# Masks added on VectorE in a fused add-and-extreme step, the causal matmuls left out, and the order table made anew

## The chip, the cores and the metric

The kernel runs on one core of a Trainium2 chip. The metric is the device time of one execution in microseconds (us): the median of three runs before the change is 4441.46 us (4438.94 to 4445.67). All five engines matter here: PE (TensorE, the matmuls), DVE (VectorE), ACT (ScalarE), POOL (GpSimd) and SP (which issues the transfers).

## The reference, cut to what matters

64 independent examples (`b`), each of 128 rows (`s`) by 256 features, pass through four layers. They hold five attentions of 16 heads, numbered 0 to 4 in the kernel: attention 0 is causal, attention 2 adds a mask that is an input of the kernel.

```
def _mha(x, kv, Wq, Wk, Wv, mask, causal):          # attentions 0 (causal) and 1
    ...
    energy = jnp.einsum('bhsk,bhtk->bhst', Q, K)
    lengths = jnp.sum(energy[:, :, 0, :] != 0, axis=-1)
    energy = jnp.where(cols[None, None, None, :] >= lengths[:, :, None, None], -jnp.inf, energy)
    if causal:
        energy = jnp.where(cols[None, :] > cols[:, None], -jnp.inf, energy)
    score = jax.nn.softmax(energy / jnp.sqrt(dk), axis=-1)
    ...
# layer 1 (attention 2, heads 64 wide, rotary, then a gated MLP)
scores = jnp.einsum('bhqd,bhkd->bhqk', q, k) / math.sqrt(HD)
scores = scores + attention_mask
probs = jax.nn.softmax(scores, axis=-1)
...
# layer 2 (attention 3): plain softmax.  layer 3 (attention 4): scaled, clipped at +-50, softmax
```

## The kernel before, in words

All weights stay in SBUF. Each example is a chain of about 85 steps ("events"), from the transposition of its input (`xT`) to its last normalization (`norm` 4). Every event is named by a name, the attention or layer `a` and, where an attention is cut in four units of four heads, the unit `u`: `scores` is the product of queries and keys of all 16 heads on PE; `soft` the maximum (DVE) and the exponential (ACT) of one unit; `turn` the transposition of one unit's probabilities (PE) and its copy (ACT); `values` the product with the values; `attended` the transposition back (PE) and the division by the sums (DVE); `first_row` finds the length penalty (`pen`); `prob_norm` divides the probabilities of attention 2 (reciprocal on DVE, product on POOL); `kv2`, `q2`, `o2`, `gate`, `up`, `down`, `z`, `h` are the projections of the layers.

Four examples are under way at once (four slots of every buffer). The order is written out by hand: the table `LIFE` (from L76) gives each event a number for each engine that takes part, and `order(engine)` (L170) sorts the events of all examples by `PERIOD * b + number`. `PERIOD` and the numbers only set this order. On each engine the instructions run strictly in it; between engines there are semaphores. So in the middle of the run the same sequence comes again for each example, on each engine, with steps of four examples interleaved. Of PSUM, four banks (`scores_ps`) hold the scores of one attention, and four (`gen_ps`) go round for all else: a step on PE waits until the bank that was filled four steps earlier has been read.

The masking of attention 0 on PE: `scores` (L519) first multiplies the identity by a bfloat16 table of the causal mask, four matmuls of 512 columns (L537); then come the penalties (16 matmuls, L542) and the scores (L563) into the same banks. In `scores_out` (L932) DVE takes the maximum of one unit (128x512, four heads) straight from PSUM, negated, for attentions 0, 1 and 3 (L957); for attention 2 it adds the mask into `masked` in SBUF (L944) and takes the maximum from there (L946). In `exponentials` (L708) ACT reads attention 0, 1 and 3 from PSUM (L724) and attention 2 from `masked` (L721), head by head, with the negated maximum as its bias. `masked` has three places, and DVE waits on each unit for the exponential of three units earlier (`exp_done`). The score banks are free for the next attention when the last unit is `scored` (after attentions 2 and 4) or `exp_done` (after 0, 1 and 3).

Of the kernel before, what the change touches and what calls it, by code (L numbers as in the profile page):

```python
# [73 lines left out]
PERIOD = 66.01  # L74

LIFE = [  # L76
    ("xT", 0, 0, {"PE": 0.00, "ACT": 2.67, "DVE": 14.33}),
# [1125 lines left out]
```

## Time and profile before

| | |
|---|---|
| profiled execution | 4448.31 us |
| its span, first to last instruction | 4446.5 us |
| PE busy | 4086.8 us (92%) |
| DVE busy | 2928.1 us (66%) |
| ACT busy | 2694.5 us (61%) |
| POOL busy | 1233.9 us (28%) |
| granted TensorE clock | 0.990 of full speed |
| chain that ended last | PE 42%, DVE 40%, issue 10%, POOL 5% |

Busy is the share of the span in which an engine works; the rest is waiting for others. The chain that ended last is followed back from the last instruction, at each step to what released it. Transfers play no part after the start: they move 53 MB in all, at 12 GB/s on average.

### The profile page before, as it was taken

What the parts mean: (1) busy time and instruction counts of PE and PEld (TensorE: products, weight loads), DVE (VectorE), ACT (ScalarE), POOL (GpSimd) and SP (SyncE); (2) the same over time, 40 slices, a digit from 0 to 9 for tenths busy, and PEclk for the clock granted to TensorE, in tenths of its full rate; (3) what the DMA queues carried; (4) which work ended last, traced back from release to release, by engine and by line L of the source; (5) the groups of instructions that cost most, each with busy time, mean ns of one, the idle gap of its engine ahead of it and who ended that gap; (6) DMA issues with size and microseconds to landing.
All of it is one profiled execution on the core that took longest, in us unless ns stands there. A gap on an engine that the chain in (4) does not pass through costs nothing.

```text
span 4446.5 us, 116614 instructions
## 1 busy us (share of the span) xinstructions
PE 4086.8 (92%) x45024; PEld 3473.5 (78%) x45024; DVE 2928.1 (66%) x7395; ACT 2694.5 (61%) x8513; POOL 1233.9 (28%) x2247
## 2 busy tenths in 40 slices
PE   4899999999999999999999999999999999999996
PEld 3778778787787787787787887787787877877875
DVE  2576676676666666766766766766766766766664
ACT  2566666656656656656656666666666666566563
POOL 0232322322322322323323323323223223223221
PEclk8999999999999999999999999999999999999998
DMA  3000000000000000000000000000000000000000
GB/s 122 1 11 7 11 11 6 11 11 7 11 11 6 11 11 6 11 11 7 11 9 8 11 6 11 11 6 11 11 6 11 11 6 11 11 6 11 11 3 5
DMA packets 47341, 52.92 MB, mean 12 GB/s; under 512 B 5328, under 2 KB 46288, under 8 KB 46416
## 3 DMA queue, kind: packets, MB, share of 16 engines
q1 hardware_dynamic: 46800, 45.46, 3.2%
q8 instruction: 369, 6.05, 0.5%
q14 instruction: 172, 1.41, 0.1%
HBM read 37.05 MB, written 8.39 MB: 10 GB/s over the span
## 4 chain that ended last, share of the span: by engine, by line
PE 42%; DVE 40%; issue 10%; POOL 5%; ACT 2%; DVEq 0%; DMA 0%; POOLq 0%; ACTq 0%
PE gen_ps L481 25%; PE gen_ps L473 9%; DVE negmax L957 4%; DVE masked L944 4%; POOL rstd L779 4%; DVE masked L951 4%; PE gen_ps L598 3%; DVE st L919 2%; DVE xs L929 2%; DVE zn L914 2%; ACT prob L724 2%; PE gen_ps L587 2%; PE scores_ps L556 2%; DVE negmax L946 2%; PE scores_ps L563 1%
## 5 line engine op out<-in xcount | busy, mean ns | idle before, releaser
L481 PE MATMUL gen_ps<-actT,w_sb 128*128 128x128 f32 x11264 | 1394.5, 277 | 3.4 <-ACT actT L694 3.3
L481 PEld LDWEIGHTS gen_ps<-actT,w_sb 128*128 128x128 f32 x11264 | 1325.8, 193 | 23.0 <-ACT actT L694 6.2
L724 ACT ACTIVATE prob<-scores_ps,negmax 128x128 f32<-128x128 f32 x3072 | 859.8, 406 | 330.6 <-DVE negmax L957 330.6
L779 POOL TENSOR_TENSOR rstd<-ve,consts 128x1 f32<-128x1 f32 x448 | 282.9, 631 | 1525.0 <-DVE ve L921 1000.0
L473 PE MATMUL gen_ps<-consts,prob 128*128 128x128 f32 x4096 | 591.0, 279 | 65.1 <-ACT prob L724 63.1
L694 ACT ACTIVATE probT<-gen_ps 128x512 f32<-128x512 f32 x1024 | 585.8, 638 | 59.7 <-PE gen_ps L473 59.7
L473 PEld LDWEIGHTS gen_ps<-consts,prob 128*128 128x128 f32 x4096 | 467.8, 142 | 184.9 <-ACT prob L724 147.2
L957 DVE TENSOR_REDUCE negmax<-scores_ps 128x4 f32<-128x512 f32 x768 | 492.0, 682 | 82.7 <-PE scores_ps L563 82.2
L481 PE MATMUL gen_ps<-w_sb,actT 128*128 128x256 f32 x2048 | 532.3, 383 | 2.7 <-ACT actT L694 1.9
L481 PE MATMUL gen_ps<-w_sb,wide 128*128 128x256 f32 x2048 | 467.9, 381 | 1.2 <-issue 1.2
L694 ACT ACTIVATE actT<-gen_ps 128x256 f32<-128x256 f32 (+1 forms) x576 | 276.5, 480 | 301.4 <-PE gen_ps L473 294.0
L832 POOL TENSOR_SCALAR prob<-prob,rden 128x128 f32<-128x128 f32 x1024 | 363.4, 376 | 233.4 <-DVE rden L987 233.4
L481 PEld LDWEIGHTS gen_ps<-w_sb,wide 128*128 128x128 f32 x2048 | 378.9, 190 | 55.6 <-ACT wide L694 1.6
L721 ACT ACTIVATE prob<-masked,negmax 128x128 f32<-128x128 f32 x1024 | 396.3, 394 | 0.0
L481 PEld LDWEIGHTS gen_ps<-w_sb,actT 128*128 128x128 f32 x2048 | 353.0, 193 | 31.7 <-ACT actT L694 3.6
L694 ACT ACTIVATE oT<-gen_ps 128x512 f32<-128x512 f32 x256 | 152.1, 594 | 347.2 <-PE gen_ps L587 347.2
L951 DVE TENSOR_TENSOR masked<-scores_ps,mask 128x512 f32<-128x512 f32 x256 | 175.7, 686 | 175.5 <-PE scores_ps L556 175.4
L716 ACT ACTIVATE probT<-masked 128x512 f32<-128x512 f32 x256 | 161.7, 632 | 212.5 <-DVE masked L954 212.4
L587 PE MATMUL gen_ps<-probT,v 128*32 128x128 f32 x8192 | 279.9, 278 | 11.0 <-ACT probT L716 6.5
L587 PEld LDWEIGHTS gen_ps<-probT,v 128*32 128x32 f32 x8192 | 210.4, 110 | 59.2 <-ACT actT L694 20.2
L787 POOL TENSOR_TENSOR res<-zn,xs 128x256 f32<-128x256 f32 x64 | 46.6, 727 | 737.7 <-DVE zn L914 737.7
L473 PE MATMUL gen_ps<-consts,zn 128*128 128x128 f32 x640 | 132.3, 289 | 127.9 <-DVE zn L914 77.3
(125 smaller groups left out, 5737.9 us busy)
## 6 DMA issues: line engine op xcount, KB each, us to landing
ctx_rms<-x_dram SPq DMA_DIRECT2D x64, 128.0 KB, 2.2
ctx<-ctx_dram SPq DMA_DIRECT2D x64, 128.0 KB, 2.2
mask<-mask_dram SPq DMA_DIRECT2D x128, 64.0 KB, 2.0
out_dram<-res SPq DMA_DIRECT2D x64, 128.0 KB, 1.7
w_sb<-weights_dram SPq DMA_DIRECT2D x1, 7680.0 KB, 25.9
w_sb<-weights_dram SPq DMA_DIRECT2D x1, 2048.0 KB, 30.3
rows_sb<-rows_dram SPq DMA_DIRECT2D x1, 1408.0 KB, 8.2
consts<-consts_dram SPq DMA_DIRECT2D x1, 460.5 KB, 3.3
```

The source lines that it names most:

```text
L473: last = nc.tensor.transpose(ps[:, k * P:(k + 1) * P], src, ident)
L481: last = nc.tensor.matmul(ps, lhsT(c), rhs(c), start=(c == 0), stop=(c == chunks - 1))
L587: last = nc.tensor.matmul(ps[32 * k:32 * k + 32, u * S:(u + 1) * S], v16[:, b % G, HU * u + k, :], probT[:, u, k, :], start=True, stop=True)
L694: release(nc.scalar.activation(dst, take(act, name, b)[:, 0:width], ACT.Copy), name, b)
L716: nc.scalar.activation(probT[:, N % 4, :, :], masked[:, N % 3, :, :], ACT.Exp).then_inc(sem("exp_done"), 1)
L721: ins = nc.scalar.activation(prob[:, N % 4, k, :], masked[:, N % 3, k, :], ACT.Exp, bias=negmax[:, N % 4, k:k + 1], accum_out=den[:, N % 4 ...
L724: ins = nc.scalar.activation(prob[:, N % 4, k, :], scores_ps[:, u, k * S:(k + 1) * S], ACT.Exp, bias=negmax[:, N % 4, k:k + 1])
L779: nc.gpsimd.tensor_tensor(dst, src, const("expo")[:, 0:width], ALU.pow)\
L832: ins = nc.gpsimd.tensor_scalar(prob[:, N % 4, k, :], prob[:, N % 4, k, :], rden2[:, N % 4, k:k + 1], 0.0, ALU.mult, ALU.add)
L944: link(nc.vector.tensor_tensor(masked[:, N % 3, :, :], ps, mask1[:, g, :].unsqueeze(1).to_broadcast([P, HU, S]), ALU.add))
L951: link(nc.vector.tensor_tensor(masked[:, N % 3, :, :], ps, fT[:, g, :].unsqueeze(1).to_broadcast([P, HU, S]), ALU.mult))
L957: ins = nc.vector.tensor_reduce(negmax[:, N % 4, :], ps, AX.X, ALU.max, negate=True)
```

## The change

For attentions 0 and 2 DVE now works head by head: one fused instruction computes -(scores + mask) for 128x128 elements, writes it to `masked` and gathers its minimum, which is the negated maximum of the masked scores and goes to `negmax`. The mask is the causal table for attention 0 and the input's mask for attention 2. ACT takes the exponential of both from `masked`, with the scale -1. The causal matmuls and their bfloat16 tables go; the first penalty matmul of a bank now starts the sum in it. The score banks are also free at `scored` after attention 0. All numbers of the order table are new; two of its lines stand for them here.

```diff
-PERIOD = 66.01
+PERIOD = 68.67
 LIFE = [
-    ("soft", 0, 0, {"ACT": 40.04, "DVE": 32.01}),
+    ("soft", 0, 0, {"ACT": 45.98, "DVE": 51.83}),
 ...
-                eng.wait_ge(sem("scored") if last in (2, 4) else sem("exp_done"), U * k)
+                eng.wait_ge(sem("exp_done") if last in (1, 3) else sem("scored"), U * k)
 ...
-                if a == 0:
-                    for r in range(R):
-                        nc.tensor.matmul(scores_ps[:, r, :], identb[:, :],
-                                         causalb[:, :].unsqueeze(1).to_broadcast([P, HU, S]),
-                                         start=True, stop=False, skip_group_check=True)
                 for k in range(HU if a < 2 else 0):
                     for r in range(R):
                         nc.tensor.matmul(scores_ps[:, r, k * S:(k + 1) * S], pick[rows_of(r), k, :],
-                                         pen[rows_of(r), g, :], start=(a == 1 and k == 0), stop=False,
+                                         pen[rows_of(r), g, :], start=(k == 0), stop=False,
 ...
-                    if a == 2:
+                    if a == 0:
                         ins = nc.scalar.activation(prob[:, N % 4, k, :], masked[:, N % 3, k, :], ACT.Exp,
+                                                   bias=negmax[:, N % 4, k:k + 1], scale=-1.0)
+                    elif a == 2:
+                        ins = nc.scalar.activation(prob[:, N % 4, k, :], masked[:, N % 3, k, :], ACT.Exp, scale=-1.0,
                                                    bias=negmax[:, N % 4, k:k + 1], accum_out=den[:, N % 4, k:k + 1])
 ...
-                if a == 2:
-                    if u == 0:
+                if a in (0, 2):
+                    if a == 2 and u == 0:
                         dve.wait_ge(mask1_sem(b), 16 * (b // G + 1))
-                    link(nc.vector.tensor_tensor(
-                        masked[:, N % 3, :, :], ps, mask1[:, g, :].unsqueeze(1).to_broadcast([P, HU, S]), ALU.add))
-                    ins = nc.vector.tensor_reduce(negmax[:, N % 4, :], masked[:, N % 3, :, :], AX.X, ALU.max,
-                                                  negate=True)
+                    for k in range(HU):
+                        ins = nc.vector.tensor_tensor_reduce(
+                            out=masked[:, N % 3, k, :], in0=ps[:, k, :], in1=mask1[:, g, :] if a else const("causal"),
+                            scale=-1.0, scalar=3.4e38, op0=ALU.add, op1=ALU.min,
+                            accum_out=negmax[:, N % 4, k:k + 1])
```

In the order, place one: DVE at `soft` of attention 2, before. L860 is the end of `norm` 0, L987 the reciprocal of `prob_norm`, L908 begins `attended` 3.

```order
L860 TENSOR_SCALAR live<-absmax 128x1
L944 TENSOR_TENSOR masked<-scores_ps,mask 128x512
L946 TENSOR_REDUCE negmax<-masked 128x4
L944 TENSOR_TENSOR masked<-scores_ps,mask 128x512
L946 TENSOR_REDUCE negmax<-masked 128x4
L944 TENSOR_TENSOR masked<-scores_ps,mask 128x512
L946 TENSOR_REDUCE negmax<-masked 128x4
L944 TENSOR_TENSOR masked<-scores_ps,mask 128x512
L946 TENSOR_REDUCE negmax<-masked 128x4
L987 RECIPROCAL rden<-den 128x4
L908 RECIPROCAL rden<-gen_ps 128x16
L914 TENSOR_TENSOR zn<-gen_ps,rden 128x256
```

Each unit is an addition and a reduction.

The same place now, its first unit only (L854 is the old L860). ISA is the fused instruction, and the second ISA, of 128x1, the read of what it gathered.

```order
L854 TENSOR_SCALAR live<-absmax 128x1
L939 ISA masked,negmax<-scores_ps,mask 128x128
L939 ISA negmax 128x1
L939 ISA masked,negmax<-scores_ps,mask 128x128
L939 ISA negmax 128x1
L939 ISA masked,negmax<-scores_ps,mask 128x128
L939 ISA negmax 128x1
L939 ISA masked,negmax<-scores_ps,mask 128x128
L939 ISA negmax 128x1
L993 BN_STATS cst<-ctx 128x6
L994 BN_AGGR cmv<-cst 128x2
L995 TENSOR_SCALAR cve<-cmv 128x1
```

Two instructions a unit have become eight, with `ctx_norms` (L993 on) moved in between the units.

Place two: PE from `queries` and `keys` of attention 1 (the second and third row) to its scores (L563), before. The row with `zn` is `zT` 3, the one with `mask` `mask4`, the one with `q` `first_row` 1, the 128x256 behind it `o` 3, the ones with `prob` `turn` 2, and `xs` and `ctx` `tr` 4.

```order
L473 MATMUL gen_ps<-consts,ctx_rms 128x128 x2
L481 MATMUL gen_ps<-actT,w_sb 128x128 x8
L481 MATMUL gen_ps<-w_sb,actT 128x256 x2
L473 MATMUL gen_ps<-consts,zn 128x128 x2
L473 MATMUL gen_ps<-consts,mask 128x128
L481 MATMUL gen_ps<-plainT,q 128x128 x2
L481 MATMUL gen_ps<-w_sb,actT 128x256 x2
L473 MATMUL gen_ps<-consts,prob 128x128 x8
L473 MATMUL gen_ps<-consts,xs 128x128 x2
L473 MATMUL gen_ps<-consts,ctx 128x128 x2
L542 MATMUL scores_ps<-pen,pick 128x128 x16
L563 MATMUL scores_ps<-plainT,wide 128x128 x16
```

The same place now (L477 is the old L481, L469 the old L473, L533 and L554 are the old L542 and L563).

```order
L477 MATMUL gen_ps<-actT,w_sb 128x128 x8
L477 MATMUL gen_ps<-w_sb,actT 128x256 x2
L469 MATMUL gen_ps<-consts,mask 128x128
L477 MATMUL gen_ps<-actT,w_sb 128x128 x4
L477 MATMUL gen_ps<-w_sb,actT 128x256 x2
L469 MATMUL gen_ps<-consts,zn 128x128 x2
L469 MATMUL gen_ps<-consts,prob 128x128 x4
L477 MATMUL gen_ps<-plainT,q 128x128 x2
L477 MATMUL gen_ps<-w_sb,actT 128x256 x2
L469 MATMUL gen_ps<-consts,prob 128x128 x4
L533 MATMUL scores_ps<-pen,pick 128x128 x16
L554 MATMUL scores_ps<-plainT,wide 128x128 x16
```

`tr` 4 has moved behind the scores, `keys` 0 (the fourth and fifth row) ahead of `turn` 2, `zT` 3 directly ahead of it, and one unit of `turn` 2 now stands ahead of `first_row` 1, which was first.

Place three: PE from the scores of attention 0 to `zT` 4, before. The row with `probT` is `values` 4, the one with `xs` `x2T`, the one of 20 the second halves of `gate` and `up` and `h`, the 128x256 behind it `z`, the one with `oT` `attended` 4, with `prob` `turn` 0, with `wide` `down`, with `zn` `zT` 4.

```order
L537 MATMUL scores_ps<-causalb,identb 128x512 x4
L542 MATMUL scores_ps<-pen,pick 128x128 x16
L563 MATMUL scores_ps<-plainT,wide 128x128 x16
L587 MATMUL gen_ps<-probT,v 32x128 x16
L473 MATMUL gen_ps<-consts,xs 128x128 x2
L481 MATMUL gen_ps<-actT,w_sb 128x128 x20
L481 MATMUL gen_ps<-w_sb,actT 128x256 x2
L473 MATMUL gen_ps<-consts,oT 128x128 x4
L473 MATMUL gen_ps<-consts,prob 128x128 x4
L481 MATMUL gen_ps<-w_sb,wide 128x256 x8
L473 MATMUL gen_ps<-consts,zn 128x128 x2
L473 MATMUL gen_ps<-consts,prob 128x128 x12
```

The same place now (L578 is the old L587).

```order
L533 MATMUL scores_ps<-pen,pick 128x128 x16
L554 MATMUL scores_ps<-plainT,wide 128x128 x16
L469 MATMUL gen_ps<-consts,xs 128x128 x2
L477 MATMUL gen_ps<-actT,w_sb 128x128 x12
L578 MATMUL gen_ps<-probT,v 32x128 x16
L477 MATMUL gen_ps<-w_sb,actT 128x256 x2
L477 MATMUL gen_ps<-w_sb,wide 128x256 x8
L469 MATMUL gen_ps<-consts,prob 128x128 x4
L469 MATMUL gen_ps<-consts,oT 128x128 x4
L469 MATMUL gen_ps<-consts,prob 128x128 x8
L469 MATMUL gen_ps<-consts,zn 128x128 x4
```

The four causal matmuls are gone, the second half of `gate` has moved ahead of the scores, and `values` 4 from directly behind them to behind `h`. `zT` 4 (the first two of the last row's four) now follows two units of `turn` 0 behind `attended` 4, where `down` lay between them.

## Rows read from the trace of the kernel before

**Rows 1.** Busy time in one period, all engines: stretch, length, then busy (count) by engine

```profile
2000.00:2067.24 67.24, 63.11 (x705) 53.76 (x703) 45.55 (x116) 42.05 (x133) 19.24 (x36) 1.00 0.03 9
```

**Rows 2.** Timeline of PE in that period: start us, us, engine, line, what, count

```profile
...
1999.63 0.59 PE L481 MATMUL gen_ps<-w_sb,actT 128*128 128x256 f32 x2
...
2014.11 1.04 PE L473 MATMUL gen_ps<-consts,prob 128*128 128x128 f32 x8
...
2015.85 0.40 PE L542 MATMUL scores_ps<-pen,pick 32*128 32x128 bf16 x16
2016.09 1.11 PE L563 MATMUL scores_ps<-plainT,wide 32*128 32x128 f32 x32
...
2022.11 3.69 PE L481 MATMUL gen_ps<-w_sb,wide 128*128 128x256 f32 x16
2025.64 1.05 PE L481 MATMUL gen_ps<-actT,w_sb 128*128 128x128 f32 x8
...
2027.39 0.60 PE L473 MATMUL gen_ps<-consts,prob 128*128 128x128 f32 x4
...
2038.26 1.02 PE L537 MATMUL scores_ps<-causalb,identb 128*128 128x512 bf16 x4 [0.22 <-DVE masked L954]
...
2052.06 0.38 PE L473 MATMUL gen_ps<-consts,zn 128*128 128x128 f32 x2
...
2066.43 1.03 PE L481 MATMUL gen_ps<-w_sb,actT 128*128 128x256 f32 x4
...
```

**Rows 3.** Groups by line: a 128x128 DVE operation, and ACT's copy of a turn

```profile
L694 ACT ACTIVATE probT<-gen_ps 128x512 f32<-128x512 f32 x1024 | 585.8, 638 | 59.7 <-PE gen_ps L473 59.7
...
L1069 DVE TENSOR_SCALAR mask<-gen_ps 128x128 f32<-128x128 f32 x64 | 16.8, 262 | 2.3 <-PE gen_ps L473 1.9 <-issue 0.4
```

**Rows 4.** Timeline of DVE: context statistics, `stats` and `norm` 0, first units of `soft` 2

```profile
...
2001.89 0.42 DVE L998 BATCH_NORM_STATS2 cst<-ctx 128x6 f32<-128x256 f32 x1
...
2002.98 0.42 DVE L919 BATCH_NORM_STATS2 st<-res 128x6 f32<-128x256 f32 x1
...
2003.64 0.15 DVE L921 TENSOR_SCALAR ve<-mv 128x1 f32<-128x1 f32 x1
2003.72 0.47 DVE L926 SCALAR_TENSOR_TENSOR zn<-res,mv,rows_sb 128x256 f32<-128x256 f32 x1
...
2005.78 0.69 DVE L944 TENSOR_TENSOR masked<-scores_ps,mask 128x512 f32<-128x512 f32 x1
2006.51 0.69 DVE L946 TENSOR_REDUCE negmax<-masked 128x4 f32<-128x512 f32 x1
2007.11 0.68 DVE L944 TENSOR_TENSOR masked<-scores_ps,mask 128x512 f32<-128x512 f32 x1
...
```

**Rows 5.** Timeline of ACT: one exponential of attention 2 and its accumulator read

```profile
...
2010.06 0.39 ACT L721 ACTIVATE prob<-masked,negmax 128x128 f32<-128x128 f32 x1
2010.35 0.19 ACT L721 ACTIVATION_READ_ACCUMULATOR prob<-masked,negmax 128x1 f32 x1
...
```

**Rows 6.** Timeline of POOL: one unit of `prob_norm`, and the residual of attention 0

```profile
...
2011.33 1.43 POOL L832 TENSOR_SCALAR prob<-prob,rden 128x128 f32<-128x128 f32 x4 [2.38 <-DVE rden L987]
...
2061.93 0.90 POOL L787 TENSOR_TENSOR res<-zn,ctx_rms 128x256 f32<-128x256 f32 x1 [3.88 <-DVE zn L914]
...
```

**Rows 7.** Timeline of DVE: `rms_norm` 3, `soft` 4 from its start, `attended` 1, `gate`

```profile
...
2027.66 0.35 DVE L1033 TENSOR_SCALAR zn<-xs,rstd 128x256 f32<-128x256 f32 x1 [0.67 <-POOL rstd L779]
...
2032.45 0.69 DVE L951 TENSOR_TENSOR masked<-scores_ps,mask 128x512 f32<-128x512 f32 x1 [2.75 <-PE scores_ps L556]
...
2038.03 0.25 DVE L908 RECIPROCAL rden<-gen_ps 128x16 f32<-128x16 f32 x1
...
2038.93 0.68 DVE L1047 SCALAR_TENSOR_TENSOR wide<-wide,gen_ps 128x512 f32<-128x512 f32 x1
...
```

**Rows 8.** Timeline of DVE: `z` (L1018), and behind the statistics of `down` (L1028)

```profile
...
2049.57 0.41 DVE L1018 TENSOR_TENSOR zn<-gen_ps,rows_sb 128x256 f32<-128x256 f32 x1
...
2053.88 0.14 DVE L1028 TENSOR_SCALAR ve<-ssq 128x1 f32<-128x1 f32 x1
...
```

More of the change, by code:

```diff
@@ new lines @@
+    ("xT", 0, 0, {"PE": 4.90, "ACT": 0.00, "DVE": 14.42}),
+    ("queries", 0, 0, {"PE": 6.89, "DVE": 23.79}),
+    ("keys", 0, 0, {"PE": 14.26, "ACT": 10.23}),
+    ("first_row", 0, 0, {"PE": 41.02, "DVE": 42.31}),
+    ("scores", 0, 0, {"PE": 44.51}),
+    ("soft", 0, 0, {"ACT": 45.98, "DVE": 51.83}),
+    ("soft", 0, 1, {"ACT": 46.67, "DVE": 51.90}),
+    ("turn", 0, 0, {"PE": 46.95, "ACT": 49.73}),
+    ("soft", 0, 2, {"ACT": 47.48, "DVE": 59.39}),
+    ("soft", 0, 3, {"ACT": 47.82, "DVE": 59.43}),
@@ new lines @@
+    ("turn", 0, 1, {"PE": 48.63, "ACT": 50.50}),
+    ("turn", 0, 2, {"PE": 50.73, "ACT": 51.63}),
+    ("turn", 0, 3, {"PE": 57.83, "ACT": 56.51}),
+    ("values", 0, 0, {"PE": 65.66, "ACT": 66.07}),
+    ("attended", 0, 0, {"PE": 67.18, "DVE": 80.19, "POOL": 78.71}),
+    ("tr", 1, 0, {"PE": 75.56, "ACT": 72.47}),
+    ("queries", 1, 0, {"PE": 78.34, "DVE": 96.15}),
+    ("keys", 1, 0, {"PE": 79.83, "ACT": 78.89}),
+    ("stats", 0, 0, {"DVE": 83.14, "POOL": 79.94}),
+    ("norm", 0, 0, {"DVE": 83.32, "POOL": 81.65}),
@@ new lines @@
+    ("ctx_norms", 0, 0, {"DVE": 89.28, "POOL": 85.92}),
+    ("first_row", 1, 0, {"PE": 88.61, "DVE": 100.10}),
+    ("soft", 1, 0, {"ACT": 90.43, "DVE": 101.65}),
+    ("soft", 1, 1, {"ACT": 91.80, "DVE": 102.99}),
+    ("scores", 1, 0, {"PE": 92.99}),
+    ("soft", 1, 2, {"ACT": 94.28, "DVE": 103.76}),
+    ("soft", 1, 3, {"ACT": 96.15, "DVE": 103.79}),
+    ("turn", 1, 0, {"PE": 98.71, "ACT": 96.31}),
+    ("turn", 1, 1, {"PE": 101.49, "ACT": 97.84}),
+    ("turn", 1, 2, {"PE": 102.86, "ACT": 98.28}),
@@ new lines @@
+    ("attended", 1, 0, {"PE": 110.13, "DVE": 112.23, "POOL": 99.30}),
+    ("turn", 1, 3, {"PE": 105.06, "ACT": 100.42}),
+    ("stats", 1, 0, {"DVE": 113.53, "POOL": 101.40}),
+    ("values", 1, 0, {"PE": 108.38, "ACT": 101.66}),
+    ("z", 1, 0, {"PE": 114.11, "DVE": 130.69, "POOL": 101.98}),
+    ("mean_square", 2, 0, {"DVE": 131.57, "POOL": 106.40}),
+    ("x2T", 1, 0, {"PE": 113.35, "ACT": 109.58}),
+    ("h", 1, 0, {"PE": 113.71, "ACT": 115.14}),
+    ("norm_x3", 1, 0, {"ACT": 116.60, "DVE": 131.37}),
@@ new lines @@
+    ("norm", 1, 0, {"DVE": 118.41}),
+    ("tr", 2, 0, {"PE": 120.48, "ACT": 124.32}),
+    ("q2", 2, 0, {"PE": 127.72, "DVE": 137.89}),
+    ("q2", 2, 1, {"PE": 133.76, "DVE": 146.44, "POOL": 133.30}),
+    ("kv2", 2, 0, {"PE": 134.43, "DVE": 148.47, "POOL": 138.93}),
+    ("rms_norm", 2, 0, {"DVE": 134.80}),
+    ("scores", 2, 0, {"PE": 142.41}),
+    ("soft", 2, 0, {"ACT": 143.54, "DVE": 155.68}),
+    ("soft", 2, 1, {"ACT": 144.47, "DVE": 158.69}),
+    ("soft", 2, 2, {"ACT": 145.68, "DVE": 161.16}),
@@ new lines @@
+    ("up", 3, 1, {"PE": 182.23, "DVE": 190.24}),
+    ("tr", 3, 0, {"PE": 190.09, "ACT": 191.80}),
+    ("queries", 3, 0, {"PE": 192.36, "DVE": 204.65}),
+    ("keys", 3, 0, {"PE": 196.30, "ACT": 197.89}),
+    ("soft", 3, 0, {"ACT": 200.57, "DVE": 207.68}),
+    ("soft", 3, 1, {"ACT": 201.39, "DVE": 208.34}),
+    ("scores", 3, 0, {"PE": 202.32}),
+    ("norm_x4", 3, 0, {"DVE": 203.97}),
+    ("turn", 3, 0, {"PE": 205.12, "ACT": 205.86}),
+    ("soft", 3, 2, {"ACT": 205.52, "DVE": 215.31}),
+    ("soft", 3, 3, {"ACT": 205.68, "DVE": 215.97}),
@@ L177 @@
+    ("norm", 4, 0, {"DVE": 273.47}),
 ]
@@ L230, in build @@
         consts = sb("consts", [P, C_ALL])
-        identb = sb("identb", [P, P], bf16)
-        causalb = sb("causalb", [P, P], bf16)
         qbias = sb("qbias", [P, 2, C])
```

140 lines of the change are left out of this document (39 added, 101 removed).

## The prediction

> **What bounds the kernel now.** I read the busy times of one period first, then PE's timeline, because PE has the least idle time. Between two equal steps on PE, the end of `kv2` at 2000.22 us (1999.63 + 0.59) and at 2067.46 (2066.43 + 1.03), lie 67.24 us [rows 2]. In such a stretch PE is busy 63.11 us, DVE 45.55, ACT 42.05, POOL 19.24, at a granted clock of 1.00 [rows 1]. So PE is nearly the bound, with 4.1 us of waits per example, and neither DVE nor ACT is short of time in sum. What counts is whether a long stretch of DVE work stands in PE's way. A table of order decides that, and here it is new, so I laid the six legs of the period of the new order out by the durations of the old one.
>
> The legs on PE, before [rows 2]: (1) end of `kv2` to `turn` 2, 2000.22 to 2014.11, 13.89; (2) to the penalties of attention 1 at 2015.85, 1.74; (3) to the end of `o2` at 2025.80 (2022.11 + 3.69), 9.95; (4) to the scores of attention 0 at 2038.26, 12.46; (5) to `zT` 4 at 2052.06, 13.80; (6) to the next end of `kv2`, 15.40.
>
> **The parts of the change.** *Causal matmuls gone.* They take 1.02 us of PE per example [rows 2], 65 us over 64 examples, all of it on PE's path.
>
> *The fused instruction.* The trace has none, so I bound it. A DVE instruction of 128x512 starts 0.60 us before the next, though its record lasts 0.69 [rows 4]; a 128x128 one lasts 0.262 [rows 3]. The difference of the records is 0.42 for 384 columns, so a 128-column instruction should let the next start after 0.60 - 0.42 = 0.18 to 0.20. The read behind it is a one-column instruction, and such a one lets its successor start after 0.08 (2003.64 to 2003.72) [rows 4]. Lower bound: the read costs nothing, T = 0.20 a head. Upper bound: both are done one after the other to their ends, 0.262 + 0.15 [rows 3, 4] and two gaps, T = 0.47. Between them lies what ACT does with the same pair: its read starts 0.29 after the exponential although that lasts 0.39 [rows 5], so the read doesn't wait for the end. I take T = 0.30: 0.20 + 0.08 and 0.02 for a slightly late read. A unit of four heads is then 1.20 us. Before, a unit of attention 2 took 1.33 (2005.78 to 2007.11) [rows 4] and one of attention 0 only 0.60, the reduction. DVE gains 0.5 and loses 2.4 us per example, 1.9 in sum; its load rises to 47.5 of 67 us. That would be hidden if the units didn't lie in a chain that PE waits for.
>
> The Trainium skill (Vector Engine (DVE) Microarchitecture Reference, section 5.2) gives 1.04 ns per column and about 75 ns per instruction after overlap; by it T would be an estimated 0.284, and the sum below 67.1 instead of 67.6. The 0.60 of rows 4 agrees with it (0.533 + 0.075).
>
> *ACT.* Attention 0 is now read from SBUF, as attention 2 was at 0.39 each [rows 5]; ACT has 25 us of idle time in a period [rows 1] and this isn't on the path. *Free banks earlier.* Attention 3 is next after 0 and comes over 10 us later on PE, so this brings nothing.
>
> *The order, leg by leg.* (Steps of 0.1 to 0.9 us without a row of their own are estimates from the durations of like instructions here.) Leg 1: DVE starts behind `kv2` at 0.1: three instructions of 256 columns (0.33 each, by the slope above) and `attended` 0 (0.56 and 0.42 to its end), 2.1. POOL adds the residual, 0.90 [rows 6], to 3.1. `stats` and `norm` 0 take 2002.98 to 2005.78, 2.80 [rows 4], to 5.9. Then `soft` 2, 16T, and three things now put between its units: `ctx_norms` 1.09 (2001.89 to 2002.98) [rows 4], `queries` 0 about 0.9 (a 128x512 instruction and a short one with its wait), `attended` 3 0.61 (0.90 of rows 7 less the product with `live`). Then the reciprocal 0.26, POOL 1.43 [rows 6], and 0.12 to PE. Leg 1 = 10.3 + 16T, 15.1. PE's own work there is about 13.1, so PE waits 2 us in front of `turn` 2. Before, `ctx_norms` came ahead of `norm`, where PE had more to do.
>
> Leg 2: `turn` 0.5, `first_row` 0.7, the penalty on DVE 1.45, 0.1 to PE: 2.75. `turn` now comes ahead of `first_row`. Leg 3: the same steps as before plus `keys` 4, 1.75 (2025.64 to 2027.39) [rows 2], and `tr` 4, 0.6: 12.3. Leg 4: DVE's `rms_norm` started 1.86 after `o2` (2027.66) [rows 7]. ACT now copies a `turn` first (a record of 0.64 [rows 3]), so 2.5, plus 0.27 to the next instruction. Then `soft` 4 with `first_row` 0 inside, 5.58 (2032.45 to 2038.03), `attended` 1, 0.90, put between them [rows 7], and `stats` 1, 0.74 (2002.98 to 2003.72) [rows 4], and `gate`, 0.60, too; 0.23 to PE: 10.8. PE could be there after 9.8; it waits 1 us. Leg 5: penalties and scores 1.35 (2015.85 to 2017.20) [rows 2], `soft` 0 with 16T and `gate` and `up`, 1.2, then `z`, `norm_x3` and `down`, 4.31 (2049.57 to 2053.88) [rows 8], 0.73 more since `mean_square` now waits for ACT ahead of `down`, `attended` 4 and the way to PE 0.86, and 0.1: 8.55 + 16T, 13.35. Before, PE had `down` to do between `attended` 4 and `zT` 4; now its own work takes about 11.7 and it waits 1.6. Leg 6: 15.40 less two `turn`s 0.95, `attended` 0 0.44, and the wait for `norm_x4`, 0.76, with 0.05 for what is left of it: 13.3.
>
> **The sum.** The parts free of T are 10.3 + 2.75 + 12.3 + 10.8 + 8.55 + 13.3 = 58.0 us, and 32T comes on top: 67.6 us with T = 0.30, against 67.24. That is 0.36 x 64 = +23 us. The balance lies at T = 0.289; each hundredth of T is 0.32 us a period and 20 us in all. The profiled execution took 4448.3 us (span 4446.5) and would take 4471; the median of the runs is 4441.5, 0.15% lower, so I predict **4464 us**. Start and end of the run I leave as they are: the period pays for both.
>
> So the causal matmuls' 1.0 us is PE time that turns into waits: PE's busy time should fall to 62.1 and its idle time rise from 4.1 to 5.5 us a period.
>
> **The rivals.** *A, the forecast,* T of 0.28 to 0.32: 67.0 to 68.2 us, 4424 to 4506 us; chance 0.50, of which 0.15 is faster, 0.11 within and 0.24 slower.
>
> *B, the read waits for the fused instruction's result.* Then it starts after 0.26 to 0.28 and the next head 0.08 later, T = 0.35: 69.2 us, +125, 4567 us. For it: DVE's own instructions with a wait between them follow their predecessor's end by 0.03 to 0.04 (2006.51 after 2005.78 + 0.69) [rows 4]. Against it: ACT's read [rows 5]. If the next head waits for the end of the read's record too, T is 0.26 + 0.15 = 0.41 without gaps and 0.47 with them: 71.1 to 73.0 us, 4690 to 4810. Chance 0.22 for the first and 0.04 for the second. The Trainium skill (VectorE: DVE Perf Modes, "The DRAIN you can't avoid") lets the next instruction start only when the pipe is empty, which is the second. Records of DVE end 0.09 behind the start of the next [rows 4], so the trace doesn't agree as far as these records go.
>
> *C, faster: PE stays the bound.* If the fused pair costs 0.25 or less, or the chains of legs 1 and 5 start earlier than I laid them (each depends on five or six handovers of about 0.1), PE's own 62.1 us shows, and waits of 3.8 us stay: 65.9 us, -85, 4356 us. With T = 0.20 the sum is 64.4, 4260 us. For it: PE was the bound in 94% of the period [rows 1]. It decides from T below 0.28, or 0.7 us less in the chains. Chance 0.24: faster 0.22, within 0.02.
>
> **Numbers.** What a measurement of this kernel can tell from no change is 0.2%, 9 us. Faster: 0.15 + 0.22 = 0.37; within: 0.11 + 0.02 = 0.13; slower: 0.24 + 0.26 = 0.50. The range takes in C at 4356 and B at 4567 with little beyond: 4345 to 4600; what stays outside is the dearest B and the cheapest C. The likeliest case's own range is 4424 to 4506.
>
> **What the profile after would show.** The fused instruction and its read: start to start 0.30 a head, 1.2 us a unit; the period between two ends of `kv2`, 67.6 us; PE busy 62.1 of it; PE waiting about 2 us for POOL's `prob` in front of `turn` 2, 1 us for `masked` of attention 4 in front of the scores of attention 0, and 1.6 us for DVE's `zn` of attention 4 in front of `zT` 4. A pair at 0.35 or more would give B. If PE's waits in these three places are short and the pair still takes 0.30, my legs are wrong, not the price.

## The result, and the profile after

The changed kernel took **4307.36 us** (median of 4 runs, 4304.02 to 4310.38), the kernel before 4442.45 us on the same chip (4438.94 to 4445.67): a ratio of 0.9696, 95% interval 0.9679 to 0.9713. That is 135 us or 3.0% faster. The forecast was 4464 us with a range of 4345 to 4600, so it had the wrong sign, and the time lies below the range.

The first view is the page of the kernel after: the span, the busy time of each engine, and from its list of costly groups the new instructions and ACT's exponentials (count after the x, then busy us and mean ns of one, then the idle time ahead of them).

```profile
span 4306.2 us, 119430 instructions
...
PE 4007.5 (93%) x44768; PEld 3474.5 (81%) x44768; DVE 2876.9 (67%) x10721; ACT 2731.0 (63%) x8513; POOL 1226.6 (28%) x2247
...
L715 ACT ACTIVATE prob<-masked,negmax 128x128 f32<-128x128 f32 x1024 | 395.3, 394 | 0.2
...
L712 ACT ACTIVATE prob<-masked,negmax 128x128 f32<-128x128 f32 x1024 | 318.4, 396 | 6.2 <-DVE negmax L939 6.2
...
L939 DVE CUSTOM_DVE_ANT_0 masked<-scores_ps,mask 128x128 f32<-128x128 f32 x1024 | 236.2, 287 | 21.3 <-DVE q L875 15.5
...
L939 DVE CUSTOM_DVE_ANT_0 masked<-scores_ps,consts 128x128 f32<-128x128 f32 x1024 | 225.7, 285 | 6.8 <-PE scores_ps L554 3.8
```

Next the busy times of one period of the kernel after, in the columns of [rows 1].

```profile
2003.00:2068.10 65.10, 61.90 (x702) 53.81 (x701) 44.79 (x168) 42.63 (x134) 19.12 (x35) 1.00 0.04 10
```

The period is 65.1 us instead of 67.24. PE's busy time fell by 1.2 us, as foreseen (62.1 was), but its idle time fell as well, from 4.1 to 3.2 us, where 5.5 was foreseen. DVE's load is 44.8 us: it fell by 0.8, where it was to rise by 1.9.

The steps that bound the six legs, in PE's timeline of that period (start, length, what; in brackets the idle time ahead and who ended it). They answer to [rows 2]: end of `kv2`, `turn` 2, penalties of attention 1, `o2`, penalties of attention 0, `zT` 4, end of `kv2`.

```profile
2003.52 1.03 PE L477 MATMUL gen_ps<-w_sb,actT 128*128 128x256 f32 x4
...
2018.34 0.65 PE L469 MATMUL gen_ps<-consts,prob 128*128 128x128 f32 x4
...
2021.23 0.41 PE L533 MATMUL scores_ps<-pen,pick 32*128 32x128 bf16 x16 [0.48 <-DVE pen L895]
...
2029.47 3.62 PE L477 MATMUL gen_ps<-w_sb,wide 128*128 128x256 f32 x16
...
2043.80 0.40 PE L533 MATMUL scores_ps<-pen,pick 32*128 32x128 bf16 x16 [0.64 <-DVE masked L949]
...
2056.11 0.70 PE L469 MATMUL gen_ps<-consts,zn 128*128 128x128 f32 x4 [0.64 <-DVE zn L908]
...
2068.61 1.03 PE L477 MATMUL gen_ps<-w_sb,actT 128*128 128x256 f32 x4
```

PE's waits over the whole run of the kernel after (us in total, times, the longest):

```profile
PE gen_ps L469 <- DVE zn L908: 69.8, 128, 2.0
PE scores_ps L533 <- DVE masked L949: 37.6, 61, 0.7
PE gen_ps L469 <- issue: 34.4, 55, 5.2
PE scores_ps L533 <- DVE pen L895: 31.0, 57, 1.7
```

On average these are waits of 0.54 to 0.63 us. In front of `turn` 2, where 2 us were foreseen, PE has nothing in brackets; it starts 0.13 us after the end of the step ahead (2017.83 + 0.38).

The term that decided stands on DVE. The first unit of attention 2 in its timeline, to be laid beside [rows 4]:

```profile
2010.46 0.29 DVE L939 CUSTOM_DVE_ANT_0 masked<-scores_ps,mask 128x128 f32<-128x128 f32 x1
2010.68 0.08 DVE L939 DVE_READ_ACCUMULATOR2_ANT negmax<- 128x1 f32 x1
2010.68 0.29 DVE L939 CUSTOM_DVE_ANT_0 masked<-scores_ps,mask 128x128 f32<-128x128 f32 x1
2010.89 0.09 DVE L939 DVE_READ_ACCUMULATOR2_ANT negmax<- 128x1 f32 x1
...
2011.31 0.08 DVE L939 DVE_READ_ACCUMULATOR2_ANT negmax<- 128x1 f32 x1
2011.31 0.42 DVE L993 BATCH_NORM_STATS2 cst<-ctx 128x6 f32<-128x256 f32 x1
```

A fused instruction starts 0.21 us after the last one, and the read of its accumulator starts in the same instant as the next fused instruction: it has no turn of its own between them. A unit of four heads is 0.85 us (2010.46 to 2011.31), where I had reckoned with 1.20.

### The profile page after: what moved, and what is told of

Its sections match the earlier page's. It is cut to its first block, busy times and chain, and to the rows that moved or that the text cites. A ratio compares the mean times of both kernels' runs of the same rounds, so it can differ in the third digit from the quotient of the medians.

```text
span 4306.2 us, 119430 instructions
## 1 busy us (share of the span) xinstructions
PE 4007.5 (93%) x44768; PEld 3474.5 (81%) x44768; DVE 2876.9 (67%) x10721; ACT 2731.0 (63%) x8513; POOL 1226.6 (28%) x2247
## 4 chain that ended last, share of the span: by engine, by line
PE 50%; DVE 33%; issue 7%; POOL 6%; ACT 4%; DVEq 0%; DMA 0%; POOLq 0%; ACTq 0%
PE gen_ps L477 31%; PE gen_ps L469 7%; DVE masked L939 5%; PE scores_ps L554 4%; DVE masked L946 4%; PE gen_ps L578 3%; POOL rstd L773 3%; PE gen_ps L589 3%; DVE st L913 2%; DVE masked L949 2%; POOL prob L826 2%; DVE xs L923 1%; DVE zn L908 1%; ACT res L762 1%; PE scores_ps L533 1%
## 5 line engine op out<-in xcount | busy, mean ns | idle before, releaser
L477 PE MATMUL gen_ps<-actT,w_sb 128*128 128x128 f32 x11264 | 1423.6, 279 | 13.0 <-ACT actT L685 6.2
L477 PEld LDWEIGHTS gen_ps<-actT,w_sb 128*128 128x128 f32 x11264 | 1330.9, 193 | 126.1 <-ACT actT L685 75.6
L685 ACT ACTIVATE probT<-gen_ps 128x512 f32<-128x512 f32 x1024 | 606.7, 623 | 333.1 <-PE gen_ps L469 332.8
L773 POOL TENSOR_TENSOR rstd<-ve,consts 128x1 f32<-128x1 f32 x448 | 268.3, 599 | 1849.2 <-DVE ve L915 978.5
L718 ACT ACTIVATE prob<-scores_ps,negmax 128x128 f32<-128x128 f32 x2048 | 571.5, 415 | 197.2 <-DVE negmax L952 197.2
L469 PE MATMUL gen_ps<-consts,prob 128*128 128x128 f32 x4096 | 596.7, 277 | 20.0 <-ACT prob L718 6.2
L469 PEld LDWEIGHTS gen_ps<-consts,prob 128*128 128x128 f32 x4096 | 476.8, 142 | 84.4 <-POOL prob L826 25.7
L477 PE MATMUL gen_ps<-w_sb,actT 128*128 128x256 f32 x2048 | 539.4, 386 | 2.4 <-ACT actT L753 1.4
L477 PE MATMUL gen_ps<-w_sb,wide 128*128 128x256 f32 x2048 | 463.2, 379 | 0.0
L952 DVE TENSOR_REDUCE negmax<-scores_ps 128x4 f32<-128x512 f32 x512 | 328.8, 684 | 198.7 <-ACT prob L718 114.1
L477 PEld LDWEIGHTS gen_ps<-w_sb,wide 128*128 128x128 f32 x2048 | 384.3, 190 | 49.7 <-issue 0.2
L715 ACT ACTIVATE prob<-masked,negmax 128x128 f32<-128x128 f32 x1024 | 395.3, 394 | 0.2
L477 PEld LDWEIGHTS gen_ps<-w_sb,actT 128*128 128x128 f32 x2048 | 353.1, 193 | 43.4 <-issue 12.3
L712 ACT ACTIVATE prob<-masked,negmax 128x128 f32<-128x128 f32 x1024 | 318.4, 396 | 6.2 <-DVE negmax L939 6.2
L578 PE MATMUL gen_ps<-probT,v 128*32 128x128 f32 x8192 | 278.4, 277 | 26.4 <-ACT probT L685 21.3
L578 PEld LDWEIGHTS gen_ps<-probT,v 128*32 128x32 f32 x8192 | 211.2, 110 | 74.0 <-issue 44.0
L939 DVE CUSTOM_DVE_ANT_0 masked<-scores_ps,mask 128x128 f32<-128x128 f32 x1024 | 236.2, 287 | 21.3 <-DVE q L875 15.5
L1036 DVE TENSOR_TENSOR xs<-gen_ps,xs 128x256 f32<-128x256 f32 x64 | 27.2, 425 | 332.5 <-PE gen_ps L477 332.5
L939 DVE CUSTOM_DVE_ANT_0 masked<-scores_ps,consts 128x128 f32<-128x128 f32 x1024 | 225.7, 285 | 6.8 <-PE scores_ps L554 3.8
```

The lines of the kernel that those rows point to most:

```text
L469: last = nc.tensor.transpose(ps[:, k * P:(k + 1) * P], src, ident)
L477: last = nc.tensor.matmul(ps, lhsT(c), rhs(c), start=(c == 0), stop=(c == chunks - 1))
L578: last = nc.tensor.matmul(ps[32 * k:32 * k + 32, u * S:(u + 1) * S], v16[:, b % G, HU * u + k, :], probT[:, u, k, :], start=True, stop=True)
L685: release(nc.scalar.activation(dst, take(act, name, b)[:, 0:width], ACT.Copy), name, b)
L712: ins = nc.scalar.activation(prob[:, N % 4, k, :], masked[:, N % 3, k, :], ACT.Exp, bias=negmax[:, N % 4, k:k + 1], scale=-1.0)
L715: ins = nc.scalar.activation(prob[:, N % 4, k, :], masked[:, N % 3, k, :], ACT.Exp, scale=-1.0, bias=negmax[:, N % 4, k:k + 1], accum_out= ...
```

## Experiments

The kernel before took 4441.4 to 4442.0 us beside them. T is the time of one fused head, start to start. "Theory 1" in the expectations is, unless they say otherwise, that T is 0.211 us and not 0.30, and that my legs hold.

**Is it T? Padding each head.** Without another form of the fused instruction, T can only be raised. One DVE copy of one column, of a buffer nobody waits for, was put ahead of each fused instruction; the second and third run have it in attention 2 or attention 0 alone.

```diff
                     for k in range(HU):
+                        nc.vector.tensor_copy(scratch[:, N % 8, k:k + 1], consts[:, k:k + 1])
                         ins = nc.vector.tensor_tensor_reduce(
```

Both attentions:

> The changed kernel with a one-column copy on DVE ahead of each fused instruction, 32 per example, so that a head costs about 0.285 us instead of 0.21. Theory 1 (both groups of units lie in chains that PE waits for, each hundredth of a us a head is 0.32 us a period): +2.4 us a period, +150 us, about 4457 us. Theory 3 (PE is the bound and DVE, 67% busy, hides it): within 20 us of 4307.

Attention 2 alone:

> The changed kernel with the one-column copy (0.062 us by the trace of the kernel with all 32) only ahead of the 16 fused instructions of attention 2. Theory 1 (leg 1 is a DVE chain with 0.1 us of slack at most): 0.9 to 1.0 us a period, +55 to +63 us, 4362 to 4370 us. Rival (the two groups count alike): half of the 95 us, 4355 us.

Attention 0 alone:

> The same copy only ahead of the 16 fused instructions of attention 0. Theory 1 (in leg 5 DVE waits 0.31 us for PE's `z`, so the first 0.3 us cost nothing): 0.6 us a period, +32 to +42 us, 4339 to 4349 us. Rival (alike): 4355 us.

Measured with both: 4402.08 us, ratio 0.9911 (0.9896 to 0.9926). DVE's timeline of that run:

```profile
2021.65 0.15 DVE L940 COPY scratch<-consts 128x1 f32<-128x1 f32 x1
2021.73 0.28 DVE L941 CUSTOM_DVE_ANT_0 masked<-scores_ps,consts 128x128 f32<-128x128 f32 x1
2021.93 0.08 DVE L941 DVE_READ_ACCUMULATOR2_ANT negmax<- 128x1 f32 x1
2021.93 0.15 DVE L940 COPY scratch<-consts 128x1 f32<-128x1 f32 x1
```

That is 95 us more than the kernel after, where the expectation had 150 (4457 us). DVE's work on this path is not hidden, which rules out theory 3 of the expectation, but the size was missed by 55 us. The head is now about 0.273 us, so the copy costs 0.062 and not the 0.075 that the expectation was worked out with; over 32 heads and 64 examples this is 27 us of the 55. The sum of the forecast gives 58.0 + 32 x 0.273 = 66.7 us, and the period was 66.6; as the same sum is 0.34 us short without the copies (table below), this near hit is in part luck.

Attention 2 alone: 4368.45 us (ratio 0.9833, 0.9818 to 0.9848), as expected, 61 us more than the kernel after, or 0.95 us a period: 16 heads x 0.062 are 0.99. It shows in leg 1 in two waits of PE that the kernel after doesn't have there, ahead of `keys` 0 and in front of `turn` 2:

```profile
2041.34 1.13 PE L478 MATMUL gen_ps<-actT,w_sb 128*128 128x128 f32 x8 [0.82 <-DVE zn L909]
...
2043.93 0.66 PE L470 MATMUL gen_ps<-consts,prob 128*128 128x128 f32 x4 [0.29 <-POOL prob L827]
```

Attention 0 alone: 4349.14 us (0.9789, 0.9773 to 0.9806), at the upper end of what was expected, 42 us more, 0.65 a period, a third of a microsecond short of the 0.99. The reason stands in DVE's timeline of the kernel after, behind the last unit of attention 0:

```profile
2049.91 0.08 DVE L939 DVE_READ_ACCUMULATOR2_ANT negmax<- 128x1 f32 x1
2050.31 0.42 DVE L1013 TENSOR_TENSOR zn<-gen_ps,rows_sb 128x256 f32<-128x256 f32 x1 [0.31 <-PE gen_ps L477]
```

DVE has to wait 0.31 us for PE's `z`. Leg 5 has a floor there: the first 0.02 us by which a head of attention 0 grows (0.31 over 16 heads) are free, and the last 0.02 on the way down from the 0.30 of the forecast brought nothing. The floor is 20 us of the 55 above. The last 8 us stay open: the two attentions alone cost 61 + 42 = 103 us, both together 95.

**Code or order? The two halves of the change.** The new code with the old table of order (two lines of the table are shown), and the old code with the new table:

```diff
-PERIOD = 68.67
+PERIOD = 66.01
 LIFE = [
-    ("soft", 0, 0, {"ACT": 45.98, "DVE": 51.83}),
+    ("soft", 0, 0, {"ACT": 40.04, "DVE": 32.01}),
 ...
```

> The changed code with the order table of before. Theory 1 (the chains of legs: a fused head costs 0.21 us, DVE's units of attention 2 shrink by 1.9 us per example, PE loses the causal 1.0 us): in the old order PE's 1.2 us wait for `zn` in front of `zT` 3 goes and the causal matmuls' 1.0 us with it, while attention 0's units cost DVE 1.0 us more and may add to the 0.8 us wait in front of `tr` 3. Period 65.0 to 66.0 us, 4300 to 4365 us. Theory 2 (the new table brings the gain): no better than 4400 us.

> The code of before with the new order table. Theory 1: units of attention 2 take 1.33 instead of 0.85 us (+1.9 a period), those of attention 0 0.60 instead of 0.85 (-1.0), and the causal matmuls stand in the chain from `soft` 4 over the scores to `soft` 0 (+1.0): 67.0 us a period, about 4430 us. Theory 2 (the table is what is better): the gain stays but for the causal matmuls, about 4372 us.

The new code in the old order took 4454.14 us (ratio 1.003, 1.0018 to 1.0041), the old code in the new order 4482.6 us (1.009, 1.0075 to 1.0106). Theory 1 was missed both times. Theory 2 fits the first time, no better than 4400 us, but its claim that the new table brings the gain is ruled out by the second. Each half alone makes the kernel slower, by 13 and 41 us, and together they gain 135. Some of PE's waits in a period of the first (new code, old order):

```profile
2013.15 0.41 PE L469 MATMUL gen_ps<-consts,zn 128*128 128x128 f32 x2 [0.48 <-DVE zn L908]
...
2043.31 0.44 PE L469 MATMUL gen_ps<-consts,xs 128*128 128x128 f32 x2 [1.50 <-DVE xs L923]
...
2045.68 2.92 PE L477 MATMUL gen_ps<-actT,w_sb 128*128 128x128 f32 x24 [0.15 <-DVE wide L1049]
...
2055.29 0.63 PE L469 MATMUL gen_ps<-consts,prob 128*128 128x128 f32 x4 [0.41 <-DVE xs L1054]
2057.53 0.44 PE L469 MATMUL gen_ps<-consts,zn 128*128 128x128 f32 x2 [0.75 <-DVE zn L1059]
```

In the kernel before, the transpose of row `x2T` 1 waited like this:

```profile
2042.13 0.44 PE L473 MATMUL gen_ps<-consts,xs 128*128 128x128 f32 x2 [0.55 <-DVE xs L929]
```

The 1.02 us of the causal matmuls are gone, and this wait has grown by 0.95: there PE only waits longer for the normalised row, which doesn't come sooner. The cheaper units of attention 2 do show a little: in front of `zT` 3 PE waited 1.17 us before, now 0.48, and 0.23 in front of the step behind it. But the units of attention 0 have grown from 0.60 to 0.85 us, and the waits of 0.15 and 0.41 us for DVE above are new. The old code in the new order waits at leg 1:

```profile
2028.32 1.13 PE L481 MATMUL gen_ps<-actT,w_sb 128*128 128x128 f32 x8 [1.03 <-DVEq L885]
...
2033.33 0.66 PE L473 MATMUL gen_ps<-consts,prob 128*128 128x128 f32 x4 [0.29 <-POOL prob L832]
```

Its stretch from the scores of attention 2 to the penalties of attention 1 is 15.38 us (2020.84 to 2036.22), against 13.61 in the kernel after (2007.62 to 2021.23): 1.77 us for four units of 1.33 instead of 0.85, which would be 1.92. Add 0.96 for the causal matmuls: 65.1 + 1.77 + 0.96 = 67.83, and its period was 67.8. My expectation for this run (4430) had also counted on attention 0's old units, cheaper by 0.25 us each, in leg 5; they bring nothing there, by the floor above.

**The parts of the code, in the new order.** First the causal matmuls put back with nothing else undone (the mask is then added twice):

```diff
+                if a == 0:
+                    for r in range(R):
+                        nc.tensor.matmul(scores_ps[:, r, :], identb[:, :],
+                                         causalb[:, :].unsqueeze(1).to_broadcast([P, HU, S]),
+                                         start=True, stop=False, skip_group_check=True)
 ...
-                                         pen[rows_of(r), g, :], start=(k == 0), stop=False,
+                                         pen[rows_of(r), g, :], start=(a == 1 and k == 0), stop=False,
```

> The changed kernel with the four causal matmuls put back ahead of the penalties (the mask is then added twice, on PE and on DVE, which changes no result). Theory 1: they lie in the chain from `soft` 4 to `soft` 0, so all of their 1.0 us shows: +65 us, 4372 us. Rival: PE's waits in front of the penalties and of `zT` 4, 0.6 us each, absorb them: 4310 to 4335 us.

It took 4373.23 us (0.9844, 0.983 to 0.9859), as theory 1 had it: 66 us more, all of the 64 x 1.02. Then attention 2 alone fused, with everything of attention 0 as before (causal matmuls, maximum and exponential from PSUM, later release of the banks); and attention 0 alone fused, attention 2 as before. Of each edit the part on DVE:

```diff
-                if a in (0, 2):
-                    if a == 2 and u == 0:
+                if a == 2:
+                    if u == 0:
```

> The new order with attention 2 fused, and attention 0 as in the kernel before (causal matmuls on TensorE, maximum read from PSUM, exponential from PSUM). Theory: attention 0's fused units bring the kernel only the 0.96 us of their causal matmuls per period, since leg 5 waits for TensorE's `z` either way: the period is 65.1 + 0.96 = 66.1 us, 4370 to 4378 us. Rival: the cheaper units of attention 0 shorten leg 5 as well (by 16 x (0.30 - 0.21) us or more), so that the period without them is 67.5 us or more, 4440 us or more.

```diff
+                if a == 2:
+                    link(nc.vector.tensor_tensor(masked[:, N % 3, :, :], ps, ..., ALU.add))
+                    ins = nc.vector.tensor_reduce(negmax[:, N % 4, :], masked[:, N % 3, :, :], AX.X, ALU.max,
+                                                  negate=True)
+                elif a == 0:
```

> The new order with attention 0 fused, and attention 2 as in the kernel before (an add and a reduction on VectorE). Theory: attention 2's units stand on the path between the scores of attention 2 and the penalties of attention 1, where a unit took 1.33 us before and takes 0.85 now, and cost 1.77 us per period there as in the run with the old code and the new order: 65.1 + 1.77 = 66.9 us, 4410 to 4428 us. Rival: with attention 0 fused the engines have enough slack that the later start of attention 1 is made good in leg 3 or 4: 4340 us or less.

They took 4372.46 us (0.9842, 0.9829 to 0.9856) and 4424.62 us (0.9961, 0.9947 to 0.9974). Both theories held. So in the new order the causal matmuls are worth 65 us and the units of attention 2 117 us, 182 in sum, and the run with neither lay 175 us above the kernel after. Attention 0's units themselves bring nothing: between 4373.23 us with the causal matmuls put back alone and 4372.46 with all of attention 0 as before lie 0.8 us. (The rival in the expectation for attention 2 alone had no ground: an old unit of attention 0 took 0.60 us, less than the fused one's 0.85.) The last run's waits at leg 1 show the same place as the old code in the new order:

```profile
2003.42 0.65 PE L469 MATMUL gen_ps<-consts,prob 128*128 128x128 f32 x4 [0.31 <-POOL prob L826]
...
2067.45 0.79 PE L477 MATMUL gen_ps<-actT,w_sb 128*128 128x128 f32 x5 [1.35 <-DVE zn L908]
```

**Why the old order gives nothing.** New code, old order, and the transposes of `x2T` 1 one step later on PE and ACT:

```diff
-    ("x2T", 1, 0, {"PE": 97.87, "ACT": 105.01}),
+    ("x2T", 1, 0, {"PE": 98.00, "ACT": 106.00}),
```

> The changed code with the order table of before, in which the transposition `x2T` 1 (and its copy on ACT) now comes behind the second half of `gate` instead of ahead of it. Theory 1 (in the old order the causal matmuls' 1.0 us turned into a longer wait, 1.50 instead of 0.55 us, for `norm` 1's `xs` in front of `x2T`): PE does 1.8 us of `gate` in that time and the wait goes, 0.9 to 1.5 us a period, 4360 to 4400 us. Rival (the old order is held up elsewhere, by DVE's work as a whole): 4440 us or more.

4452.94 us (1.0025, 1.0015 to 1.0035), no gain. The wait has only changed its place, as PE's timeline and DVE's show:

```profile
2046.52 2.92 PE L477 MATMUL gen_ps<-actT,w_sb 128*128 128x128 f32 x24 [1.68 <-DVE wide L1049]
```

```profile
2043.60 0.49 DVE L923 SCALAR_TENSOR_TENSOR xs<-zn,rstd,rows_sb 128x256 f32<-128x256 f32 x1 [0.51 <-POOL rstd L773]
2044.00 0.29 DVE L939 CUSTOM_DVE_ANT_0 masked<-scores_ps,consts 128x128 f32<-128x128 f32 x1
...
2045.68 0.69 DVE L1049 SCALAR_TENSOR_TENSOR wide<-wide,gen_ps 128x512 f32<-128x512 f32 x1
```

Eight fused heads, 1.68 us, stand in DVE's old order between the row `xs` and the step of `up` (L1049) that frees PE's bank. So in the next run that step was put ahead of them, with the move of `x2T` 1 kept:

```diff
-    ("up", 3, 0, {"PE": 156.33, "DVE": 166.05}),
+    ("up", 3, 0, {"PE": 156.33, "DVE": 163.80}),
```

> The new code with the old order, x2T 1 one unit later (as in the run before with that edit), and VectorE's first step of `up` 3 put ahead of the first units of `soft` 0. Theory 1: in the old order the time of the causal matmuls came back as a wait for one thing, the copies of the first half of the gate and up pass, which stood on VectorE behind eight fused instructions of `soft` 0; with that step ahead of them the wait of 1.68 us goes and nothing takes its place beyond about 0.3 us: a period of 66.0 us, 4350 to 4385 us. Rival: the wait only moves on, to the row `zT` and the normalisation behind VectorE's records of `xs`, which already stood at 0.41 and 0.75 us: 4430 us or more.

4395.36 us (0.9895, 0.9882 to 0.9909). This lies between the two bands, 10 us above the one of theory 1, and 58 us below the run ahead of it:

```profile
2017.70 2.94 PE L477 MATMUL gen_ps<-actT,w_sb 128*128 128x128 f32 x24 [0.74 <-ACT actT L685]
```

Of 1.68 us 0.74 are left, now for ACT's copy of `x2T`; the waits of 0.41 and 0.75 stayed. So of the 147 us between the old and the new order (4454 and 4307), 58 were held back at one place, which the two moves shorten; whether the waits that stayed hold back the rest was not tested, and neither was what the two moves would bring with the old code.

**A better version.** Two waits of the kernel after (0.64 us each, ahead of the scores of attention 0 and of `zT` 4) have other work before or beside them that could stand elsewhere. In the first, ACT copies a `turn` ahead of `o2`'s square:

```profile
2033.56 0.60 ACT L685 ACTIVATE probT<-gen_ps 128x512 f32<-128x512 f32 x1 [1.48 <-PE gen_ps L469]
2034.06 0.41 ACT L762 ACTIVATE res<-xs 128x256 f32<-128x256 f32 x1
```

The square was put ahead of the copy, and one more unit of `turn` 0 ahead of `zT` 4:

```diff
-    ("turn", 0, 3, {"PE": 57.83, "ACT": 56.51}),
+    ("turn", 0, 3, {"PE": 51.30, "ACT": 52.00}),
-    ("o2", 2, 0, {"PE": 170.87, "ACT": 167.47, "DVE": 173.50}),
+    ("o2", 2, 0, {"PE": 170.87, "ACT": 166.90, "DVE": 173.50}),
```

> The changed kernel with two events moved in the table: ACT squares `xs` behind `o2` ahead of the copy of `turn` 1, unit 2 (0.5 us earlier into the chain that ends 0.64 us after PE is ready for the scores of attention 0), and `turn` 0, unit 3, comes ahead of `zT` 4 on PE and ACT (0.44 us of PE work into the wait of 0.64). Theory 1: 0.9 us a period less, 4245 to 4260 us. Rival (both waits come back at the next step, since the chains run on): 4290 to 4307 us.

4255.61 us (0.9582, 0.9568 to 0.9596), as theory 1 had it. The first wait is gone, and of the second less than half is left:

```profile
2034.68 0.63 PE L469 MATMUL gen_ps<-consts,zn 128*128 128x128 f32 x4 [0.30 <-DVE zn L908]
```

Then two more on PE, `queries` 0 ahead of `tr` 1 and `first_row` 1 ahead of `turn` 2:

```diff
-    ("queries", 0, 0, {"PE": 6.89, "DVE": 23.79}),
+    ("queries", 0, 0, {"PE": 6.80, "DVE": 23.79}),
-    ("first_row", 1, 0, {"PE": 88.61, "DVE": 100.10}),
+    ("first_row", 1, 0, {"PE": 85.97, "DVE": 100.10}),
```

> The kernel with both moves of the run before (o2's square ahead of a copy of `turn` 1, a unit of `turn` 0 ahead of `zT` 4), and two moves on TensorE more: `first_row` 1 ahead of `turn` 2, and `queries` 0 ahead of `tr` 1, so that work which is ready fills the waits of 0.5 + 0.2 and 0.52 us there. Theory: TensorE is the bound, and each filled wait is a gain: about 1.0 us per period less than 4255.6, 4185 to 4205 us. Rival: the waits are of a chain through VectorE and ScalarE of that length and come back behind the moved work: 4245 to 4262 us.

**4224.59 us** (0.9509, 0.9496 to 0.9522), 4.9% faster than the kernel before and the fastest of all. It is 20 us above the band of its theory and below the rival's: the waits of 0.52 us (ahead of `tr` 1) and 0.50 us (ahead of the penalties of attention 1) are gone, but 0.42 came back behind `queries` 0:

```profile
2041.06 1.16 PE L477 MATMUL gen_ps<-actT,w_sb 128*128 128x128 f32 x8 [0.25 <-ACT actT L685]
...
2042.39 1.13 PE L477 MATMUL gen_ps<-actT,w_sb 128*128 128x128 f32 x8 [0.17 <-DVEq L879]
```

## Why the prediction was wrong

The legs measured in the kernel after, from the rows above, beside what the forecast gives with T = 0.30 and with the measured 0.211:

| leg | T = 0.30 | T = 0.211 | measured |
|---|---|---|---|
| 1, end of `kv2` to `turn` 2 | 15.1 | 13.7 | 13.79 |
| 2, to penalties of attention 1 | 2.75 | 2.75 | 2.89 |
| 3, to end of `o2` | 12.3 | 12.3 | 11.86 |
| 4, to scores of attention 0 | 10.8 | 10.8 | 10.71 |
| 5, to `zT` 4 | 13.35 | 11.9 | 12.31 |
| 6, to the next end of `kv2` | 13.3 | 13.3 | 13.53 |
| period | 67.6 | 64.75 | 65.09 |

*The step that failed is the size of T.* "I take T = 0.30: 0.20 + 0.08 and 0.02 for a slightly late read." It is 0.211: the first term was right, and the other two come to 0.01 between them. By the forecast's own sum that is 32 x 0.089 = 2.85 us a period and 182 us in all, where the miss was 157 us. Priced by the padding runs, which have the floor in them, the same 0.089 is an estimated 145 to 156 us (the period grew by 1.48 us, or by 0.95 + 0.65, for 0.062 a head; add the floor of 0.31, carry it up to 0.089 and take the floor off again). So T's size explains the miss nearly whole. The lower bound of the text, T = 0.20, was nearly it. What misled me was ACT's pair [rows 5]: its read delays the next exponential by about 0.1 us, and I took it as a pattern for DVE, whose read stands beside the next head and not ahead of it. The padding runs show that both groups of heads count: 0.062 more per head moved the time by 61 us in attention 2 and by 42 in attention 0.

*Rival C was right in its condition,* a pair at 0.25 or less, and in its sum for T = 0.20, 4260 us. Its name, "PE stays the bound", was not: a busy share of 94% [rows 1] doesn't make PE the bound. If it were, the copies on DVE would have been hidden, and they cost 95 us. Nor is DVE alone the bound, as the causal matmuls on PE cost 66. The path goes from one to the other. I gave C 0.24 and a time of 4356, and cut the range off at 4345, although its own lower end stood in the text: a bound that I had worked out from rows was left outside the range.

*The estimate from the Trainium skill* (Vector Engine (DVE) Microarchitecture Reference, section 5.2: 1.04 ns per column and about 75 ns per instruction) gave an estimated 0.284 for the pair, because I charged the read a fixed part of its own. For the fused instruction alone it gives an estimated 0.133 + 0.075 = 0.208, which agrees with the measured 0.211; the read, charged as an instruction of its own, is where this trace doesn't agree.

*Rival B* falls: a fused record lasts 0.28 to 0.29 us, and both the read and the next head start 0.21 after its start, so neither waits for its end.

*The legs held* to 0.44 us each and 0.34 in sum, the sum with some luck, as leg 3's error cancels leg 5's. Leg 3 came 0.44 us shorter than reckoned, and leg 5 0.4 longer: my chain left out that DVE's `z` needs PE, the floor of 0.31 us.

*Causal matmuls.* "1.0 us is PE time that turns into waits" was wrong in the new order: putting them back costs 66 us, all of it, as the same text had said earlier ("all of it on PE's path"). It was right for the old order, where the wait at `x2T` grew by 0.95.

*Waits.* Foreseen were 2, 1 and 1.6 us in front of `turn` 2, the scores of attention 0 and `zT` 4. They came out at 0.13, 0.64 and 0.64. Behind the first and third stand 16 heads each, and 16 x 0.089 = 1.42 less leaves 0.6 and, with the 0.3 of the floor, 0.5. Half of PE's idle time stands at four places that were not foreseen: 0.40 and 0.52 us inside leg 1, which take up the first wait, 0.48 ahead of the penalties of attention 1, and 0.26 ahead of `values` 1 in leg 4.

*ACT and banks.* The exponentials of attention 0 from SBUF take 0.396 us, as foreseen from attention 2's, and in the period no wait of PE stands behind them. The earlier release of the banks brings nothing, as foreseen: it is among what lies between 4373.23 and 4372.46 us.

*DVE's load* was to rise to 47.5 us and fell to 44.8: 32 x 0.089 = 2.85 is what explains the 2.7 between.

Left open: how much of the old order's remaining 88 us against the kernel after (4395 against 4307) belongs to which of its waits (I tried two moves only), and the 8 us by which the two padding runs don't add up.

## What to carry to other kernels

Where a sum hangs on one price times many instructions (here 32 heads a period, 20 us for each hundredth of a microsecond), carry both ends of the price through to the range, and don't borrow it from another engine's like pair. A changed instruction and a changed order are one change: cheaper work pays only where the order puts it on the path, and here either half alone lost time where both together gained. A faster step has a floor at the next input of another engine, and the wait that appears in the trace there tells its size.
